# A selective-scan kernel: fixed roles for its two job banks, an unrolled program and a widening matmul over all rows

## The reference

```python
xr, gate = split(x @ W_in.T, 2);  xr = xr + cond
xc = silu(conv4(xr) + b_conv)                     # causal, four taps, each channel by itself
xn = (xc - mean) / sqrt(var + 1e-5) * ln_g + ln_b
Bm, Cm, dt = split(xn @ W_xproj.T, 3)
dt = tanh(dt @ W_dt.T + b_dt) * 0.01
Ad = 1 + dt * -tanh(A_log);  Bd = Bm * minimum(norm(xn), 1)
h  = clip(h * Ad + Bd x xn, -10, 10)              # for each position in turn
y  = Cm . h + D * xn
out = x + (y * silu(gate)) @ W_out.T
```

## Time and profile before

| | |
|---|---|
| median of three runs | 2647.21 us |
| profiled execution, its span | 2646.32 us, 2644.5 us |
| mean granted clock | 0.924 |
| PE, PEld | 2464.8, 1640.8 us (93%, 62%) |
| DVE, ACT, POOL | 1733.8, 1163.2, 1795.0 us (66%, 44%, 68%) |
| chain that ended last | PE 69%, POOL 11%, ACT 9%, issue 8% |
| DMA | 117.43 MB in 77764 packets, mean 44 GB/s |

### The profile page before, as it was taken

One profiled execution on the slowest core, in us unless ns is written; L12 is line 12 of the kernel. 1 busy time (PEld: TensorE's weight loads), 2 busy tenths in 40 slices (PEclk: granted clock), 3 DMA queues, 4 the chain that ended last, 5 costly groups with the idle time before them and its releaser, 6 DMA issues.

```text
span 2644.5 us, 53114 instructions
## 1 busy us (share of the span) xinstructions
PE 2464.8 (93%) x18048; PEld 1640.8 (62%) x18048; DVE 1733.8 (66%) x2139; ACT 1163.2 (44%) x2570; POOL 1795.0 (68%) x1416
## 2 busy tenths in 40 slices
PE   5699999999999999999999999999999999999988
PEld 4466666666666666666666666666666666666644
DVE  4366776766766666675766766667676666757666
ACT  3344444434444444344444444444444444444442
POOL 3267776667767577676777766677675776767776
PEclk8789999989989899898999999899898998999989
DMA  4111110111111111111111101111111111111110
GB/s 141 40 47 51 37 48 22 48 51 51 38 31 39 48 51 51 35 32 37 51 52 38 47 22 47 51 51 38 30 40 47 51 51 35 34 37 49 47 47 12
DMA packets 77764, 117.43 MB, mean 44 GB/s; under 512 B 17924, under 2 KB 46980, under 8 KB 72900
## 3 DMA queue, kind: packets, MB, share of 16 engines
q1 hardware_dynamic: 77512, 113.98, 13.8%
HBM read 59.40 MB, written 9.18 MB: 26 GB/s over the span
## 4 chain that ended last, share of the span: by engine, by line
PE 69%; POOL 11%; ACT 9%; issue 8%; DVE 2%; SPq 1%; DMA 1%; POOLq 0%; DVEq 0%; ACTq 0%
PE ps_y L577 13%; PE ps_fill L550 10%; PE ps_fill L541 10%; PE ps_job L459 9%; PE ps_job L442 7%; PE ps_job L447 7%; POOL prod L1040 6%; ACT low L743 3%; POOL xc L1014 3%; PE ps_job L454 3%; PE ps_y L563 2%; ACT xr L705 2%; ACT bqm L726 2%; PE ps_job L468 1%; PE ps_job L483 1%
## 5 line engine op out<-in xcount | busy, mean ns | idle before, releaser
L1040 POOL TENSOR_TENSOR prod<-ks,crep 128x512 f32<-128x512 f32 x1024 | 1290.8, 1269 | 739.8 <-PE ps_y L577 672.3
L943 DVE TENSOR_TENSOR_SCAN ks<-low,ps_fill 128x512 f32<-128x512 f32 x1024 | 1241.5, 1216 | 683.1 <-PE ps_fill L550 649.7
L743 ACT COPY low<-ps_fill 128x512 f32<-128x512 f32 x1024 | 598.7, 585 | 986.0 <-PE ps_fill L541 980.9
L577 PE MATMUL ps_y<-c_sb,prod 128*128 128x128 f32 x4096 | 648.1, 283 | 0.9 <-POOL prod L1040 0.9
L577 PEld LDWEIGHTS ps_y<-c_sb,prod 128*128 128x128 f32 x4096 | 495.3, 147 | 139.9 <-issue 63.9
L550 PE MATMUL ps_fill<-pack,one 2*128 2x512 f16 x1024 | 408.6, 399 | 87.0 <-ACT low L743 49.4
L541 PE MATMUL ps_fill<-ts,xs 128*128 128x128 f16 x4096 | 422.3, 228 | 13.5 <-issue 8.0
L541 PEld LDWEIGHTS ps_fill<-ts,xs 128*128 128x128 f16 x4096 | 239.9, 100 | 258.5 <-issue 196.6
L550 PEld LDWEIGHTS ps_fill<-pack,one 2*128 2x128 f16 x1024 | 93.1, 91 | 362.4 <-issue 172.1
L459 PE MATMUL ps_job<-xr,diag 128*128 128x128 f32 x2048 | 279.3, 281 | 11.0 <-ACT bqm L726 7.9
L459 PEld LDWEIGHTS ps_job<-xr,diag 128*128 128x128 f32 x2048 | 250.7, 194 | 19.8 <-issue 16.0
(11 more groups left out here) (119 smaller groups left out, 2204.5 us busy)
## 6 DMA issues: line engine op xcount, KB each, us to landing
crep<-c_dram SPq DMA_DIRECT2D x32, 1024.0 KB, 5.1
xs<-xh SPq DMA_DIRECT2D x256, 62.0 KB
xs<-xl SPq DMA_DIRECT2D x224, 64.0 KB
xf<-in_xT SPq DMA_DIRECT2D x32, 256.0 KB, 4.5
res<-in_x SPq DMA_DIRECT2D x32, 256.0 KB, 4.5
out_dram<-res SPq DMA_DIRECT2D x32, 256.0 KB, 7.9
ts<-tth SPq DMA_DIRECT2D x128, 32.0 KB
ts<-tth SPq DMA_DIRECT2D x128, 31.0 KB
```

Of the source, the lines that this page charges most:

```text
L577: last = mm(ps_y[:, u // 4, cut], prod[:, s % HOLD, e, :], ident, start=False, stop=(u % 4 == 3 and q == 3 and e == QN - 1), is_transpose= ...
L743: copy(low[:, s % RING], ps_fill[:, s % RING]).then_inc(sem["low_copied"], 1)
L943: nc.vector.tensor_tensor_scan(ks[:, u % 2, QN * q:QN * (q + 1)].rearrange("d n t -> d (n t)"), low[:, s % RING], ps_fill[:, s % RING], 0. ...
L1040: tt(prod[:, i % HOLD], ks[:, u % 2, part], crep[:, p, part], ALU.mult).then_inc(sem["weighed"], 1)
```

## The change

- *Program.* The hardware loop is gone; all steps from -2 to 32 are written out.
- *Banks.* Each job has a seventh entry, its bank: `gate`, `out`, `xr` and `conv` in bank 0, all thin ones in bank 1. `bank_free` looks back for the last job with the same entry. The two lists overlap in points: `gate` stands beside `yT` and `hend`, `xr` beside `h0`, `conv` beside `carry` and `xt`. `out` has eight parts instead of five.
- *Widening.* `spans` is now 128 rows, zero but for rows 64 and 65, and `pick` is a 128 x 128 matrix with ones in these two rows. The matmul has the same 512 columns.
- *Side work.* The statistics of a step move from point 0 to point 59 of the step before, and POOL's reciprocal root with them; `xa` from 16 to 10, the casts (XH) from 23 to 16, z from 24 to 20, the x16 split from 26 to 13. The decay chain is cut into three points from 33. POOL's xn goes from s=7 to 6, the low part of x16 from 13 to 7, norm and xl from 10 to 9, xd from 9 to 11, h16 from 19 to 18. The scan of every fourth tile no longer comes after the first point's side work.
- *Storage.* `z1` and `th` are computed in place; `zeros` is a view of `spans`; `lend` is a tensor of its own.

```diff
+        lend = sb("lend", [NS, 2, DI])
+        spans = sb("spans", [P, 2, NS * P], H)
+        pick = sb("pick", [P, P], H)
+        zeros = spans[0:NS, 0, 0:2 * P].bitcast(F)
...
-        JOBS = [(0, 2, "z", 0, 1, 1), (3, 1, "yT", 0, -1, 2),
...
-                (40, 1, "nb", 0, 1, 1), (41, 1, "mb", 0, 1, 1),
-                (42, 4, "conv", 0, 2, 2), (46, 2, "carry", 0, 1, 2),
...
+        JOBS = [(0, 2, "z", 0, 1, 1, 1), (2, 4, "gate", 0, 0, 2, 0), (3, 1, "yT", 0, -1, 2, 1),
+                (6, 1, "hend", 0, -1, 2, 1), (9, 1, "hend", 1, -1, 2, 1), (9, 4, "gate", 1, 0, 2, 0),
+                (11, 1, "yT", 1, -1, 2, 1), (15, 8, "out", 0, -1, 1, 0), (22, 1, "zT", 0, 1, 1, 1),
+                (24, 1, "dt", 0, 1, 1, 1), (27, 4, "xr", 0, 2, 2, 0), (27, 1, "h0", 0, 1, 2, 1),
+                (31, 1, "h0", 1, 1, 2, 1), (34, 4, "xr", 1, 2, 2, 0), (39, 1, "nb", 0, 1, 1, 1),
+                (41, 4, "conv", 0, 2, 2, 0), (43, 2, "carry", 0, 1, 2, 1), (46, 2, "carry", 1, 1, 2, 1),
+                (48, 4, "conv", 1, 2, 2, 0), (50, 1, "xt", 0, 2, 2, 1), (53, 1, "mb", 0, 1, 1, 1),
+                (56, 1, "xt", 1, 2, 2, 1)]
...
+        STATS_AT, Z1_AT, Z2_AT, XA_AT, X16_AT, XH_AT, Z_AT = 59, 2, 4, 10, 13, 16, 20
+        CHAIN_AT = 33
...
-                mm -= 2
+                mm -= 1
...
-                _, _, name, i, off, per = JOBS[mm]
-                if exists(kk, off):
+                _, _, name, i, off, per, b = JOBS[mm]
+                if b == JOBS[m][6] and exists(kk, off):
...
-            for k in range(-2, 2):
-                body(k, k % 2)
-            with eng.Fori(2, STEPS - 2, 2) as k0:
-                body(k0, 0)
-                body(k0 + 1, 1)
-            for k in range(STEPS - 2, STEPS + 1):
+            for k in range(-2, STEPS + 1):
                 body(k, k % 2)
...
-                mm(ps_fill[:, s % RING], one2, spans[:, p, q * BANK:(q + 1) * BANK], start=False, stop=True,
+                mm(ps_fill[:, s % RING], pick[:], spans[:, p, q * BANK:(q + 1) * BANK], start=False, stop=True,
...
-                if point == 23 and exists(k, 1):
+                if point == XH_AT and exists(k, 1):
...
-                    if s == 7 and exists(k, 1):
+                    if s == 6 and exists(k, 1):
                         pool.wait_ge(sem["xa"], j + 1)
```

More of the change, by code:

```diff
@@ L419, in job @@
             def job(k, p, m, part):
-                _, parts, name, i, off, per = JOBS[m]
+                _, parts, name, i, off, per, b = JOBS[m]
                 if not exists(k, off):
@@ L602, in body @@
                     jobs_at(k, p, 2 * s + 1)
-            steps(pe, body)
+            steps(body)
         @block.scalar
@@ L638, in at @@
                     return [i for i in range(per) if LAST[name, i] == point and exists(k, off)]
-                if point == 16 and exists(k, 1):
+                if point == XA_AT and exists(k, 1):
                     j, q = k + 1, (p + 1) % 2
@@ L670, in side @@
                     act_fn(z[:, 0:NS], z[:, 0:NS], ACT.Identity, scale=tiny[:, 6:7]).then_inc(sem["zb"], 1)
-                if point == 26 and exists(k, 2):
+                if point == X16_AT and exists(k, 2):
                     act.wait_ge(sem["xT_in"], 16 * (k + 3))
@@ L755, in body @@
                         split_high(n)
-            steps(act, body)
+            steps(body)
         @block.vector
@@ L809, in side @@
                 j, q = k + 1, (p + 1) % 2
-                if point == 0 and exists(k, 1):
+                if point == STATS_AT and exists(k, 2):
+                    j = k + 2
                     dve.wait_ge(sem["xt_taken"], 2 * (j + 1))
@@ L822, in side @@
                     tsc(tiny[:, 2:3], mom[:, 0:1], -1.0, None, ALU.mult).then_inc(sem["norm_in"], 1)
-                if point == 2 and exists(k, 1):
+                    j = k + 1
+                if point == Z1_AT and exists(k, 1):
                     dve.wait_ge(sem["norm_in"], j + 1)
                     dve.wait_ge(sem["z_ready"], j + 1)
-                    stt(z1[:], sums[:, 0, :], tiny[:, 2:3], bank("z")[:, 0:3 * NS], ALU.mult, ALU.add
+                    since(dve, "zT_ready", j)
+                    since(dve, "h0_ready", 2 * j)
+                    stt(z[:], sums[:, 0, :], tiny[:, 2:3], bank("z")[:, 0:3 * NS], ALU.mult, ALU.add
                         ).then_inc(sem["z_taken"], 1)
-                if point == 7 and exists(k, 1):
+                if point == Z2_AT and exists(k, 1):
                     dve.wait_ge(sem["rstd"], j + 1)
@@ L883, in side @@
                     tsc(h1[:], h1[:], CLIP, -CLIP, ALU.min, ALU.max).then_inc(sem["h1_done"], 1)
-                if point == LAST["h0", 1] + 2 and exists(k, 1):
+                if point == CHAIN_AT and exists(k, 1):
                     nc.vector.tensor_tensor_scan(pf[:, 1, 1:], ad[:, 1:], zeros[:, 1:], 1.0,
@@ L888, in side @@
                     nc.vector.reciprocal(pf[:, 0], pf[:, 1]).then_inc(sem["recip"], 1)
+                if point == CHAIN_AT + 1 and exists(k, 1):
                     dve.wait_ge(sem["recip"], j + 1)
@@ L894, in side @@
                     tt(bc[:, q, 1], zT[:, 1], pf[:, 1], ALU.mult).then_inc(sem["weighted"], 1)
+                if point == CHAIN_AT + 3 and exists(k, 1):
+                    dve.wait_ge(sem["recip"], j + 1)
                     since(dve, "bound_out", 48 * j)
@@ L949, in body @@
                         scan(0)
-                    late = (s + 1) % NQ == 0
-                    if exists(k, 0) and s + 1 < TILES and not late:
+                    if exists(k, 0) and s + 1 < TILES:
                         scan(s + 1)
                     for point in (2 * s, 2 * s + 1):
-                        if point % 2 and exists(k, 0) and s + 1 < TILES and late:
-                            scan(s + 1)
                         if point == GATED_AT[0] and exists(k, 0):
```

67 lines of the change are left out of this document (28 added, 39 removed), and 3 rows, old and new, of the table JOBS.

## The result

| | us, median | runs | ratio to before, 95% interval |
|---|---|---|---|
| before | 2647.21 | 2646.41 to 2647.8 | |
| changed kernel | 2705.9 | 2688.92 to 2706.8 | 1.0202 [1.0166, 1.0237] |

The account below looks back on a forecast made before the run. TensorE, busy 93% of the span, was taken as the bound. Step: 76.5 - 5.3 - 3.5 - 1.0 + 6.2 + 1.65 + 2.05 = 76.6; with jumps -91, steps +3, ends -8: 2551 us, range 2380 to 2715.

Parts of the forecast that it names:

- straight program, in all: Hardware loop: thirteen jumps back at 7.0 us each vanish, 91 us in all, and straight code fetches without a stop.
- sum of slots with the full-row widening: TensorE, widening to widening: about 0.2 us less per slot, sum 71.5 to 66.2, a gain of 5.3 us a step.
- low clock around h0: TensorE at the two one-row h0 matmuls: slow clock gone once they are spread out, gain 3.5 us a step.
- A: Slots 7 to 9: ScalarE's casts wait for xn and delay a copy; PE stops 3.7 us, slow clock 2.5 more.
- B: Slots 16 to 20: VectorE's decay chain and ScalarE's bqm delay the copy for tile 22; widening 1.65 us late.
- C: Point 44, slot 22: conv and carry parts share a point, so the second carry waits; PE stands 2.05 us.
- what is outside the 29 steps: Before the first and in the last two steps: stops partly missing, widening gains 0.1 to 0.2 a slot, -8 us.
- The clock falls at all three stops: Rival: PE restarts at low clock after every stop, 4.1 us each; step 86.4, total 2835 us; chance 0.18.
- The widening gap stays: Rival: the gap belongs to the wait for ScalarE's copy; 5.3 us more a step, 2721 us; chance 0.07.
- The stops don't form: Rival: all three PE stops vanish, step 66.7, total 2261 us; chance 0.24 for stops missing in part or whole.
- they cancel: Rival: gains and losses balance within 0.2%, which is 5 us; chance 0.04.

Follow-up runs that it names:

- the quiet POOL: Changed kernel with POOL's products of tiles 15 to 20 cut to 8 columns and h16's low half to 8, waits kept: 2500.49 us, ratio 0.9447.
- the experiment with two rows: Changed kernel with the widening matmul reading only its two rows, 64 and 65, again: 2815.15 us, ratio 1.0631.
- the last version: Changed kernel with two bnd on ScalarE, bc merged, h16 later, xn earlier, casts at 17, carry before conv, nb/carry/xt points later: 2347.17 us, ratio 0.8863.

## Why the prediction was wrong

By its own steps, in us per step:

| step of the prediction | forecast | measured |
|---|---|---|
| straight program, in all | -91 | -103 |
| sum of slots with the full-row widening | 66.2 | gap 0.21, floor 1.29; slots without a stop as summed |
| low clock around h0 | gone | gone |
| A: stop, clock | 3.7, 2.5 | 3.3, 1.4 |
| **B: stop, clock** | **1.65, 0** | **5.2, 0.9** |
| C: stop, clock | 2.05, 0 | 2.2, 1.3 |
| a step | 76.6 | 81.2 |

**The step that failed is B.** It forecast the delay at 1.65 with durations of VectorE from the earlier trace rows (reciprocal at the end of 3.9, bnd at 0.34, "the four bnd take 1.75"), read in a step where POOL had one product of 1.27 us beside the chain, while the old slots 15 and 16 were slow. With the slow stretch gone and the work moved, POOL is busy for 7.13 us of it (which of the moves does how much was not tried apart). B then is 3.55 longer, 29 x 3.55 = 103 us; the quiet POOL takes all of it back. The prediction costed each instruction at one reading, and the same trace held the warning, even in that step: its last two bnd (from 1108.37) met the product and took 1.55, where they take 0.47 alone. Groups of VectorE's instructions in the kernel before:
```profile
L883 DVE TENSOR_SCALAR h<-h 16x1024 f32<-16x1024 f32 x32 | 41.0, 1282 | 1.1
...
L893 DVE TENSOR_TENSOR bc<-zT,pf 16x128 f32<-16x128 f32 x32 | 28.6, 893 | 0.0
...
L894 DVE TENSOR_TENSOR bc<-zT,pf 16x128 f32<-16x128 f32 x32 | 16.2, 508 | 0.0
```
The two bc took 1.4 on average, where the one reading gave 0.47 for both and p_end.

**The second miss is the clock behind B and C**, set to 0 since their stops are shorter than 2.9. Low clock behind them costs time in 18 and 23 of the 29 steps, 0.9 and 1.3 on average; A's was smaller than forecast by 1.1. Together 1.1 a step, 32 us. B is 5.2 in two pieces, so that a part of it follows from the first miss; C's 2.2 is a plain counterexample, since it stays with the quiet POOL, where B has gone (slots 23 and 24 at 7.59). The rest is small: A -0.4 and C +0.15 for the stops (these terms make 4.4 of the 4.6 that a step is longer than forecast), and 5 us are left for what is outside the 29 steps, where the forecast had put -8. 29 x (81.2 - 76.6) = 133, and 2551 + 133 + 5 = 2689 is the profiled execution.

**The rivals.** "The clock falls at all three stops" named the mechanism and that 79.9 a step is the point of return; but its price of 4.1 for each was too high (1.4, 0.9, 1.3), and the B in it was as short as in the forecast. "The widening gap stays" is refuted by the 0.21 and by 109 us in the experiment with two rows. The widening itself takes 0.38 in both forms, which agrees with the rule of the Trainium skill that few rows take as long as 128 (TensorE: Matmul & The Clock Gate, "Why this matters for your kernels"); what the two rows cost lies between them and their neighbours. "The stops don't form" is refuted by the waits, and "they cancel" by the 2%. "That POOL's instructions stretch VectorE's" was no rival, and should have been one: the load of both was looked at as busy time, side by side.

Open is why the clock falls behind a stop in some steps and not in others, and why at B it falls now before the last wait and now behind it: steps of 77.7 and 82 have the same stops.

## What to carry to other kernels

A duration that is read from a trace holds for the company in which it was read. Before a chain on VectorE is moved next to other POOL work, look at the same instruction's shortest and longest time, and take the longest if it meets POOL's long operations. Here two short operations of the chain moved to ScalarE, two merged into one and h16 moved away gave 100 us together. And a queue that issues transfers one after another has a latest start of its own, which becomes the bound once the compute stops are gone.

## What the runs showed of the hardware

- An instruction of one column in 16 rows took 2.19 us, until POOL's 2.35 us instruction ended; beside a POOL that does little, 16x127 operations took 0.20 to 0.40 in place of 1.19 to 1.41.
- Not every VectorE operation stretches. The reciprocal took 941 ns on average in the changed kernel, where it seldom met POOL, and 941 in the last version, where it met a product in 27 of 32 steps. The scans of ks, with one input in PSUM, took 1212 ns in the changed kernel and with the quiet POOL.
- Beside a widening on two rows there is about 0.1 us on each side that one on 128 rows, most of them zeros, does not have (a slot of 2.38 became 2.17, an empty one of 1.39 became 1.29): 109 us of a kernel with 1024 of them.
- Behind C's stop of 2.05 us the clock was at the low level in 23 of 29 steps, and in 20 of 29 with the quiet POOL. The last version waits in each step too, longest at the second carry (46.8 us in 32 times, 1.5 each), and its clock was 1.00 over 29 steps. Low clock ahead of a wait that another engine ends cost nothing (slots 19 and 20 are 10.09 us at 0.83 and 10.11 at 0.98).
